# Which queue begins the store of a batch's normalised rows: from the sync engine to GpSimd, in a decoder layer on one core

## The chip, the cores and the metric

One core of one Trainium2 chip. The metric is the device time of one execution in microseconds (us), median of the runs. The engines are TensorE (PE, with its weight loads as PEld), VectorE (DVE), ScalarE (ACT), GpSimd (POOL) and the sync engine (SP), which here only begins transfers. SPq and POOLq are the queues of transfers that SP and POOL begin.

## What is computed

A post-norm decoder layer in fp32 on x of 16 batches x 256 rows x 256 columns, with a context of 77 rows per batch:

```python
x = _layernorm(x + attn(x))               # a gated scan over the rows, 16 states
x = _layernorm(x + xattn(ctx_1024, x))    # cross attention, 8 heads of 128, keys = 77 context rows + 256 latents
x = _layernorm(x + ffn(x))                # 8 experts, top 2, at most 512 rows each
```

In the last line a row that no expert takes is only normalised: `_layernorm(x)` of the second line's result. The kernel therefore writes, for every batch, the rows of the second line normalised once more (the tile `xo`) to the output, and the experts' part overwrites the rows that an expert has taken.

## The kernel before, in words

All fp32 products are made of three matmuls on a high and a low part (lines 632 to 634). The work has two parts. The first runs over the batches b = 0 to 15, each in eight heads h; the second runs over the 8 experts. The orders of all engines are written out by hand, one function `body(b, par, have, had, tile)` for each engine, and `bodies` (line 402) calls it sixteen times. `have` says what a body does beside the attention of batch b: "nxt" the mixer's end and the first norm of batch b+1, "prv" the second norm and routing of batch b-1, "ctx" one more tile of context rows (bodies 1, 3, ... 13), "aft" the mixer's first product of batch b+2. "prv" is in the bodies 1 to 15, "nxt" in 0 to 14.

What is around the change, by engine:

- GpSimd, lines 2241 to 2333. In every head it scales the softmax's rows (`prob`, line 2250, two instructions, which wait for `rinv` of VectorE, line 1867) and copies a strip of them (2253). TensorE then transposes them (line 661). At h = 0 it scatters rows of the batch before to their slots, four indirect transfers (line 2135). At h = 3 it computes `c_rs`, `xrow` and, in lines 2277 to 2280, `xo`, after a wait that the last store of `xo` has landed (`xo_st`). At h = 4 it computes `a_rs` (`powers`, line 2157), at h = 5 the first norm of the next batch (`normalised`, 2175 and 2179), at h = 6 `latents_part` (2165, 2167), at h = 6 and 7 the routing.
- VectorE, after `a_rs`, makes `lnp` (line 1576, two instructions), which TensorE transposes (line 764).
- SP, lines 534 to 575. Its queue is strictly in order. A body loads `xts` and `xs` (539, 542), then half of the values of batch b (491 to 494), context tiles, keys, then half of the values of batch b+1 after a wait for head 3 (line 563), and last the store of `xo` (line 575), after a wait for `xo_set` (574), which line 2279 raises. The next body's loads of `xts` and `xs` stand right behind it.
- After the bodies SP loads expert weights and rows, and both SP (583) and GpSimd (2352) wait once more that all 15 stores have landed.

`xo` has one buffer, [128, 2, 256] in fp32, 256 KB; a store of it has 256 rows of 1 KB.

Of the kernel before, what the change touches and what calls it, by code (L numbers as in the profile page):

```python
# [78 lines left out]
def need(eng, sem, value):  # L79

    if isinstance(value, int) and value <= 0:
        return
    eng.wait_ge(sem, value)


def at(b, value):

    return isinstance(b, int) and b == value


def build(nc, x, xT, ctxt, in_w, xp_w, out_w, vecs, vec16, Wq, Wkv, Wo, bo, emb, W1, W2, out):
# [7 lines left out]
    with top:  # L99
# [3 lines left out]
        def sem(name):  # L103
            return top.enter_context(nc.semaphore(name))
# [34 lines left out]
        def s1(name, shape, dt=F32):  # L139
            return sb(name, shape, dt, one)  # L140
# [25 lines left out]
        xo = s1("xo", [P, NT, D])  # L166
# [89 lines left out]
        def weights_in(e):  # L256
# [71 lines left out]
        xb_set, cstat_set, crs_set, x2_set, xo_set, xo_st = (  # L328
            sem("xb_set"), sem("cstat_set"), sem("crs_set"), sem("x2_set"), sem("xo_set"), sem("xo_st"))
# [83 lines left out]
        def ap(t):  # L413
            return t.bitcast(F32)
# [9 lines left out]
        out_rows = out[0:NTOK, :].rearrange("(b t p) d -> b p t d", t=NT, p=P)  # L424
# [30 lines left out]
        def _(sp):  # L455
# [8 lines left out]
            def expert_weights(e):  # L464
                for part, w in enumerate((W1, W2)):
                    sp.dma_start(wraw[:, e - 1, part, :], w[e]).then_inc(ew_ld[e - 1], 16)

            def next_context(c):

                need(sp, cxn_set, c)  # L470
                sp.dma_start(cxs[:], ctxt[bass.ds(c, 1)].rearrange("o p d -> (o p) d")).then_inc(ctx_ld, 16)

            def keep_context(c):

                need(sp, cxl_set, c + 1)
                need(sp, cx_st, 32 * c)
                for d, part in zip(cx_tiles, (cx_hi, cx_lo)):
                    sp.dma_start(d[bass.ds(c, 1)].rearrange("o p k t -> (o p) k t"), ap(part[:])).then_inc(cx_st, 16)

            def keep_values(c):  # L480

                need(sp, vcl_set, 2 * c + 2)
                need(sp, vc_st, 32 * c)
                for d, part in zip(vc_tiles, (vst_hi, vst_lo)):
                    sp.dma_start(d[bass.ds(c, 1)].rearrange("o p n -> (o p) n"), ap(part[:])).then_inc(vc_st, 16)

            def values(a, half):

                c = slice(half * 512, half * 512 + 512)
                hi, lo = [d[bass.ds(a, 1)].rearrange("o t n -> (o t) n") for d in vc_rows]  # L490
                sp.dma_start(ap(v_hi[0:CTX, 2, c]), hi[:, c]).then_inc(vc_ld[half], 16)
                sp.dma_start(ap(v_hi[CTX:CTX + REST, 2, c]), lo[32:CTX, c]).then_inc(vc_ld[half], 16)
                sp.dma_start(ap(v_lo[0:CTX, 2, c]), hi[:, c]).then_inc(vc_ld[half], 16)
                sp.dma_start(ap(v_lo[96:P, 2, c]), lo[0:32, c]).then_inc(vc_ld[half], 16)
# [39 lines left out]
            def body(b, par, have, had, tile):  # L534
                a = b + 1
                if "aft" in have:
                    sp.wait_ge(in_mm, min(2 * (b + 2), 6))
                    need(sp, xTl_set, b - 1)
                    sp.dma_start(xts[:], xT_d[bass.ds(b + 2, 1)].rearrange("o p k s -> (o p) k s")).then_inc(xT_ld, 16)
                if "nxt" in have:  # L540
                    need(sp, xa_set, a)
                    sp.dma_start(xs[:], x_d[bass.ds(a, 1)].rearrange("o p t d -> (o p) t d")).then_inc(x_ld, 16)
                if at(b, B - 2):
                    sp.wait_ge(in_mm, 2 * B)
                    sp.dma_start(w1r, W1[0]).then_inc(w1r_ld, 16)
                    sp.dma_start(w2r, W2[0]).then_inc(w2r_ld, 16)
                if "att" in have:
                    need(sp, av_mm, 8 * b)
                    values(b, 1)
                if "ctx" in have:  # L550
                    next_context(tile + 1)
                    keep_context(tile)
                if "nxt" in have:
                    need(sp, cx_st, 32 * tile + 32)
                    need(sp, k_mm, 8 * b)
                    for d, part in zip(cx_rows, (kv_hi[1 - par], kv_lo[1 - par])):
                        sp.dma_start(ap(part[:, :, S:KEYS]), d[bass.ds(a, 1)].rearrange("o p k t -> (o p) k t")
                                     ).then_inc(kvc_ld, 16)
                if "ctx" in have:
                    keep_values(tile)  # L560
                if "nxt" in have:
                    need(sp, vc_st, 32 * tile + 32)
                    need(sp, av_mm, 8 * b + 4)
                    values(a, 0)
                if at(b, B - 1):
                    sp.wait_ge(v_mm, 4 * B)
                    expert_weights(3)
                    expert_weights(7)
                    sp.wait_ge(q_mm, 4 * B)
                    expert_weights(1)  # L570
                    expert_weights(5)
                if "prv" in have:
                    c = b - 1
                    need(sp, xo_set, 2 * c + 2)
                    sp.dma_start(out_rows[bass.ds(c, 1)].rearrange("o p t d -> (o p) t d"), xo[:]).then_inc(xo_st, 16)

            bodies(sp, body)


# [1539 lines left out]
        def _(pool):  # L2119
# [34 lines left out]
            def powers(a):  # L2154

                need(pool, astat_set, 6 * a + 6)
                pool.tensor_tensor(a_rs[:].rearrange("p c t -> p (c t)"),
                                   a_vv[:].rearrange("p c t -> p (c t)"), powm[:],
                                   ALU.pow).then_inc(ars_set, 1)
# [10 lines left out]
            def normalised(b, par):  # L2170

                a = b + 1
                need(pool, ars_set, a + 1)
                for t in range(NT):
                    pool.tensor_scalar(x1[1 - par][:, t, :], xa[:, t, :], a_mv[:, t, 0:1],
                                       a_rs[:, 0, t:t + 1], ALU.subtract, ALU.mult).then_inc(x1p_set, 1)
                need(pool, x1p_set, 2 * a + 2)
                need(pool, cvec_set, 1)
                pool.tensor_tensor(x1[1 - par][:], x1[1 - par][:],
                                   cvec[:].unsqueeze(1).broadcast_to([P, NT, D]),  # L2180
                                   ALU.add).then_inc(x1_set, 1)
# [59 lines left out]
            def body(b, par, have, had, tile):  # L2241
                for h in range(H):
# [37 lines left out]
                                               ALU.add, ALU.mult).then_inc(xo_set, 1)  # L2280
                    if h == 4 and "nxt" in have:
                        powers(a)
                    if h == 5 and "nxt" in have:
                        normalised(b, par)
                    if h == 6 and "prv" in have:
# [22 lines left out]
                    if h == 7 and "prv" in have:  # L2308
# [24 lines left out]
                        pool.tensor_copy(slot_u[:], slot_a[:].rearrange("p t c -> p (t c)")).then_inc(slot_set, 1)  # L2333

            bodies(pool, body)
            ending()

# [83 lines left out]
```

## Time and profile before

| | us |
|---|---|
| median of 3 runs | 1010.71 (1010.63 to 1012.13) |
| profiled execution, its own time | 1010.28 |
| its span, first to last instruction | 1008.5 |
| PE busy | 980.1 (97%) |
| DVE busy | 828.8 (82%) |
| ACT busy | 727.9 (72%) |
| POOL busy | 578.4 (57%) |
| mean granted TensorE clock | 0.994 |

Outside the span lie 1.8 us. A row of the timeline view is: start, duration, engine, line, operation, output<-input, how many instructions it merges, and in brackets the idle time of the engine before it and who ended it. A row of the groups view ends in busy us, mean ns of one, idle us before the group with what ended it.

### The profile page before, as it was taken

What the parts mean: (1) busy time and instruction counts of PE and PEld (TensorE: products, weight loads), DVE (VectorE), ACT (ScalarE), POOL (GpSimd) and SP (SyncE); (2) the same over time, 40 slices, a digit from 0 to 9 for tenths busy, and PEclk for the clock granted to TensorE, in tenths of its full rate; (3) what the DMA queues carried; (4) which work ended last, traced back from release to release, by engine and by line L of the source; (5) the groups of instructions that cost most, each with busy time, mean ns of one, the idle gap of its engine ahead of it and who ended that gap; (6) DMA issues with size and microseconds to landing.
All of it is one profiled execution on the core that took longest, in us unless ns stands there. A gap on an engine that the chain in (4) does not pass through costs nothing.

```text
span 1008.5 us, 21673 instructions
## 1 busy us (share of the span) xinstructions
PE 980.1 (97%) x7018; PEld 928.1 (92%) x7018; DVE 828.8 (82%) x2115; ACT 727.9 (72%) x1869; POOL 578.4 (57%) x1060
## 2 busy tenths in 40 slices
PE   8999999999999999999999999999999999999994
PEld 6789999999999999999999999999999999898993
DVE  6887878888888888887888788878888887678885
ACT  6686877777787768786778677867777676546772
POOL 4743565665565656655574647565665464535775
PEclk9999999999999999999999999999999999999997
DMA  7663031112211131104110311131112303555542
GB/s 249 194 144 108 17 110 48 52 46 75 82 52 46 46 111 52 47 15 142 47 45 7 122 35 62 36 110 48 51 46 74 116 30 125 187 168 160 171 156 98
DMA packets 63030, 88.97 MB, mean 88 GB/s; under 512 B 15540, under 2 KB 44008, under 8 KB 62920
## 3 DMA queue, kind: packets, MB, share of 16 engines
q1 hardware_dynamic: 56968, 71.10, 22.9%
q0 software_dynamic: 5952, 16.50, 4.7%
q8 instruction: 58, 0.95, 0.4%
q14 instruction: 52, 0.43, 0.1%
HBM read 49.31 MB, written 38.26 MB: 87 GB/s over the span
## 4 chain that ended last, share of the span: by engine, by line
PE 79%; ACT 7%; DVE 6%; issue 4%; POOL 2%; DMA 2%; POOLq 0%; SPq 0%; DVEq 0%; ACTq 0%
PE ps L632 21%; PE ps L634 21%; PE ps L633 20%; PE ps L661 7%; PE ps L740 3%; PE ps L676 1%; PE ps L678 1%; ACT prob L1255 1%; DVE nmx L1858 1%; PE ps L778 1%; ACT hp L1098 1%; PE ps L771 1%; POOL out L2359 1%; PE ps L764 1%; DMA cxs<-in_ctxt 1%
## 5 line engine op out<-in xcount | busy, mean ns | idle before, releaser
L2250 POOL TENSOR_SCALAR prob<-prob,rinv 128x333 f32<-128x333 f32 x256 | 143.6, 572 | 235.4 <-DVE rinv L1867 234.8
L1250 ACT ACTIVATE oT_hi<-ps 128x256 fp32r<-128x256 f32 x126 | 48.3, 383 | 150.7 <-PE ps L678 150.7
L632 PE MATMUL ps<-kv_lo,w_hi 128*128 128x256 f32 (+1 forms) x512 | 154.8, 302 | 1.1 <-DVE kv_lo L1416 1.1
L634 PE MATMUL ps<-kv_hi,w_hi 128*128 128x256 f32 (+1 forms) x512 | 152.9, 299 | 0.0
L633 PE MATMUL ps<-kv_hi,w_lo 128*128 128x256 f32 (+1 forms) x512 | 152.5, 298 | 0.0
L1255 ACT ACTIVATE prob<-ps,nmx 128x333 f32<-128x333 f32 x256 | 134.8, 537 | 7.7 <-DVE nmx L1858 7.7
L1416 DVE TENSOR_TENSOR pT_lo<-ps,pT_hi 128x512 fp32r<-128x512 f32 x254 | 130.9, 548 | 0.9 <-ACT pT_hi L1267 0.3
L1858 DVE TENSOR_REDUCE nmx<-ps 128x2 f32<-128x666 f32 x128 | 108.3, 846 | 8.8 <-PE ps L634 7.5
L661 PE MATMUL ps<-ident,prob 128*128 128x128 f32 (+1 forms) x768 | 105.7, 273 | 1.8 <-POOL prob L2250 1.0
L632 PEld LDWEIGHTS ps<-kv_lo,w_hi 128*128 128x128 f32 x512 | 96.9, 189 | 1.7 <-issue 1.5
L634 PEld LDWEIGHTS ps<-kv_hi,w_hi 128*128 128x128 f32 x512 | 96.8, 189 | 0.0
L633 PEld LDWEIGHTS ps<-kv_hi,w_lo 128*128 128x128 f32 x512 | 96.5, 188 | 0.0
L661 PEld LDWEIGHTS ps<-ident,prob 128*128 128x128 f32 (+1 forms) x768 | 89.9, 140 | 6.7 <-issue 1.6
L1477 DVE SCALAR_TENSOR_TENSOR cv<-hp,vec,cv 128x256 f32<-128x256 f32 x192 | 87.5, 474 | 1.0 <-ACT cv L1146 0.9
L632 PE MATMUL ps<-k_lo,q_hi 128*128 128x334 f32 x256 | 81.2, 317 | 2.0 <-DVE k_lo L1422 2.0
L1422 DVE SCALAR_TENSOR_TENSOR k_lo<-ps,vec,k_hi 128x334 fp32r<-128x334 f32 x128 | 71.4, 558 | 12.0 <-ACT k_hi L1077 11.5
L633 PE MATMUL ps<-k_hi,q_lo 128*128 128x334 f32 x256 | 80.6, 315 | 0.0
L634 PE MATMUL ps<-k_hi,q_hi 128*128 128x334 f32 x256 | 80.4, 314 | 0.0
L632 PE MATMUL ps<-w_lo,oT_hi 128*128 128x256 f32 x254 | 77.5, 305 | 0.2 <-DVE oT_lo L1416 0.2
L1267 ACT ACTIVATE pT_hi<-ps 128x512 fp32r<-128x512 f32 x127 | 76.9, 606 | 0.4
L2135 POOL DMA_INDIRECT slots<-xrow,slot_u x60 | 63.7, 1062 | 21.7 <-issue 20.4
L1430 DVE SCALAR_TENSOR_TENSOR q_lo<-ps,vec,q_hi 128x256 fp32r<-128x256 f32 x128 | 55.8, 477 | 24.3 <-ACT q_hi L1085 24.3
(336 smaller groups left out, 3318.2 us busy)
## 6 DMA issues: line engine op xcount, KB each, us to landing
wraw<-in_W SPq DMA_DIRECT2D x14, 512.0 KB, 5.2
vcd_hi<-vst_hi SPq DMA_DIRECT2D x10, 512.0 KB, 2.7
vcd_lo<-vst_lo SPq DMA_DIRECT2D x10, 512.0 KB, 3.5
v_hi<-vcd_hi SPq DMA_DIRECT2D x32, 154.0 KB
v_lo<-vcd_hi SPq DMA_DIRECT2D x32, 154.0 KB
slots<-initr SPq DMA_DIRECT2D x8, 522.0 KB, 9.8
xs<-in_x SPq DMA_DIRECT2D x16, 256.0 KB, 4.2
xts<-in_xT SPq DMA_DIRECT2D x15, 256.0 KB, 3.9
```

Source lines behind the costliest of these rows:

```text
L632: pe.matmul(dst, hi1, lo2, start=first, stop=False, skip_group_check=True)
L633: pe.matmul(dst, lo1, hi2, start=False, stop=False, skip_group_check=True)
L634: return pe.matmul(dst, hi1, hi2, start=False, stop=last, skip_group_check=True)
L661: last = pe.transpose(ps[0:r, far if j == 2 else T0, (j % 2) * S + t * P:(j % 2) * S + t * P + P], prob[:, ring, t, j * P:j * P + r], iden ...
L1255: act.activation(prob[:, h % 2, t, 0:KEYS], ps[:, S0 + t, 0:KEYS], ACT.Exp, bias=nmx[:, h % 2, t:t + 1], accum_out=rsum[:, h % 2, t:t + 1] ...
L1267: act.activation(pT_hi[:, 0:2, :].rearrange("p j s -> p (j s)"), ps[:, T0, :], ACT.Copy).then_inc(pTh_set, 1)
L1416: return dve.tensor_tensor(dst, src, ap(hi), ALU.subtract)
L1422: dve.scalar_tensor_tensor(out=k_lo[:, idx % 2, :], in0=g[:, 0:KCOL], scalar=vec[:, V_BK + idx:V_BK + idx + 1], in1=ap(k_hi[:, idx % 2, :] ...
L1477: op = dve.scalar_tensor_tensor(out=cv[:, ct, :], in0=hp[:, ct, k:k + S], scalar=w, in1=cv[:, ct, :], op0=ALU.mult, op1=ALU.add)
L1858: dve.tensor_reduce(nmx[:, h % 2, :], ps[:, S0:S0 + NT, 0:KEYS], AX.X, ALU.max, negate=True).then_inc(nmx_set, 1)
L2135: pool.indirect_dma_start(slots, bass.IndirectOffsetOnAxis(slot_u[:, 2 * t + c:2 * t + c + 1], 0), rows[:, t, :], None).then_inc(sc_done, 16)
L2250: pool.tensor_scalar(prob[:, h % 2, t, 0:KEYS], prob[:, h % 2, t, 0:KEYS], rinv[:, h % 2, t:t + 1], 1.0, ALU.mult, ALU.mult).then_inc(norm ...
```

## The change

GpSimd's body gets the wait and the store at h = 4, behind `powers(a)` and ahead of head 5; SP's body loses both. The tile, the destination, the semaphores and the condition ("prv") stay the same.

```diff
@@ sync, end of body
-                if "prv" in have:
-                    c = b - 1
-                    need(sp, xo_set, 2 * c + 2)
-                    sp.dma_start(out_rows[bass.ds(c, 1)].rearrange("o p t d -> (o p) t d"), xo[:]).then_inc(xo_st, 16)
@@ gpsimd, body
                     if h == 4 and "nxt" in have:
                         powers(a)
+                    if h == 4 and "prv" in have:
+                        need(pool, xo_set, 2 * b)
+                        pool.dma_start(out_rows[bass.ds(b - 1, 1)].rearrange("o p t d -> (o p) t d"), xo[:]
+                                       ).then_inc(xo_st, 16)
                     if h == 5 and "nxt" in have:
                         normalised(b, par)
```

## Rows read from the trace of the kernel before

**Rows 1.** The page: busy time of each engine, and the chain by engine.

```profile
PE 980.1 (97%) x7018; PEld 928.1 (92%) x7018; DVE 828.8 (82%) x2115; ACT 727.9 (72%) x1869; POOL 578.4 (57%) x1060
...
PE 79%; ACT 7%; DVE 6%; issue 4%; POOL 2%; DMA 2%; POOLq 0%; SPq 0%; DVEq 0%; ACTq 0%
```

**Rows 2.** The stretch of bodies 2 to 14: busy us by engine, granted clock.

```profile
150.00:820.00 670.00, 668.11 (x4880) 640.30 (x4879) 568.83 (x1427) 505.57 (x1349) 393.09 (x776) 1.00 0.20 62
```

**Rows 3.** The store's own rows: issue in ns (min/median/max), and landing.

```profile
L575 SPq DMA_DIRECT2D out<-xo x15: 423/424/453, 143.6 to 863.7; - x15
...
DMA to landing us min/median/max: 3.2/3.6/6.7
```

**Rows 4.** Timeline of SP's queue, end of body 7 and of body 8.

```profile
463.85 0.45 SPq L575 DMA_DIRECT2D out<-xo  x1
464.41 0.40 SPq L539 DMA_DIRECT2D xts<-in_xT  x1
...
500.35 0.42 SPq L575 DMA_DIRECT2D out<-xo  x1
```

**Rows 5.** Timeline of GpSimd, scatters and heads 3 to 5 of body 8.

```profile
468.97 1.14 POOL L2135 DMA_INDIRECT slots<-xrow,slot_u  x1 [0.46 <-issue]
...
471.97 0.96 POOL L2135 DMA_INDIRECT slots<-xrow,slot_u  x1 [0.30 <-issue]
...
490.75 1.09 POOL L2279 TENSOR_SCALAR xo<-xb,c_nm,c_rs 128x256 f32<-128x256 f32 x2
...
497.52 1.02 POOL L2157 TENSOR_TENSOR a_rs<-a_vv,powm 128x4 f32<-128x4 f32 x1 [3.43 <-DVE a_vv L1568]
500.87 1.22 POOL L2250 TENSOR_SCALAR prob<-prob,rinv 128x333 f32<-128x333 f32 x2 [2.33 <-DVE rinv L1867]
502.15 0.26 POOL L2253 COPY prob<-prob 128x90 f32<-128x90 f32 x1
```

**Rows 6.** Timelines of ScalarE and VectorE, first readers of xts and xs.

```profile
476.39 0.62 ACT L1138 ACTIVATE xt_hi<-xts 128x512 fp32r<-128x512 f32 x1
...
495.47 0.69 DVE L1556 TENSOR_TENSOR xa<-ps,xs 128x512 f32<-128x512 f32 x1 [0.39 <-PE ps L746]
```

**Rows 7.** Scatters and lnp: ns min/median/max.

```profile
L2135 POOL DMA_INDIRECT slots<-xrow,slot_u x60: 956/970/1262, 150.3 to 883.3; - x60
...
L1576 DVE TENSOR_SCALAR lnp<-xa,a_mv,a_rs x32: 401/406/823, 28.1 to 817.4; 128x256 f32<-128x256 f32 x32
```

**Rows 8.** Timeline of GpSimd, body 14 and body 15 (heads 4, 5).

```profile
815.40 1.02 POOL L2157 TENSOR_TENSOR a_rs<-a_vv,powm 128x4 f32<-128x4 f32 x1 [2.95 <-DVE a_vv L1568]
818.33 1.07 POOL L2250 TENSOR_SCALAR prob<-prob,rinv 128x333 f32<-128x333 f32 x2 [1.91 <-DVE rinv L1867]
...
861.96 0.26 POOL L2253 COPY prob<-prob 128x90 f32<-128x90 f32 x1
866.66 1.06 POOL L2250 TENSOR_SCALAR prob<-prob,rinv 128x333 f32<-128x333 f32 x2 [4.44 <-DVE rinv L1867]
```

**Rows 9.** Timeline of TensorE: transposes of head 5's prob, and of lnp.

```profile
504.97 0.82 PE L661 MATMUL ps<-ident,prob 128*128 128x128 f32 x6
...
500.89 0.51 PEld L764 LDWEIGHTS ps<-ident,lnp 128*128 128x128 f32 x4
```

**Rows 10.** Timelines of VectorE and GpSimd, three places where both work.

```profile
28.08 1.15 DVE L1576 TENSOR_SCALAR lnp<-xa,a_mv,a_rs 128x256 f32<-128x256 f32 x2
...
28.24 0.83 POOL L2152 TENSOR_TENSOR cx_lo<-cfull,cx_hi 128x256 fp32r<-128x256 f32 x1 [0.35 <-DVE cx_hi L1518]
...
472.18 0.48 DVE L1477 SCALAR_TENSOR_TENSOR cv<-hp,vec,cv 128x256 f32<-128x256 f32 x1
...
499.96 0.73 DVE L1576 TENSOR_SCALAR lnp<-xa,a_mv,a_rs 128x256 f32<-128x256 f32 x2
...
921.04 0.16 DVE L1895 CAST tku<-xsl 128x8 uint32<-128x8 f32 x1
...
920.92 1.08 POOL L2359 DMA_INDIRECT out<-fo,tku  x1 [1.71 <-ACT fo L1363]
```

## Prediction

> **What bounds the kernel.** I read the page's busy row and its chain first. TensorE is busy 97% of the span, GpSimd 57%; the queues SPq and POOLq hold 0% of the chain, and transfers 2% [rows 1]. Then the stretch in which 13 of the 15 moved stores lie: from 150 to 820 us TensorE is busy 668.11 of 670.00 us at the full granted clock [rows 2]. So in the batches TensorE's own work sets the end, all its idle time together is below 2 us, and no shorter path on another engine can give back more than that. Third, the timelines of the two queues that trade the instruction, and of the engines that wait behind them. The question is only whether GpSimd, once it carries the store, makes TensorE late somewhere.
>
> **What is removed.** SP begins 15 stores at 0.42 us each, 6.3 us in all; they need 3.6 us to land at the median, 6.7 us at most [rows 3]. Ahead of the store SP stands in no wait for xo: in body 8 its store starts at 500.35 us [rows 4], and xo was written by 491.84 us [rows 5], 8.5 us earlier. What stands behind it, the loads of xts and xs, starts 0.56 us after it (463.85 to 464.41) [rows 4] and can come about that much earlier. The load of xts from 464.41 us is first read by ScalarE at 476.39 us, 12 us later, and that of xs, right behind it, by VectorE at 495.47 us, 31 us later [rows 6]. An earlier start changes neither, and TensorE has nearly no idle time to give back. Gain: 0.
>
> **What is added.** Fifteen times GpSimd gets one wait and one transfer at head 4, behind a_rs. The wait is for its own xo, written at 491.84 us; a_rs ends at 498.54 us [rows 5], so it never holds. No plain transfer is begun by GpSimd in this trace, so its price is bounded from both sides. The nearest rows are its indirect ones: 0.97 us at the median for a scatter of 128 rows of about the same length, 0.96 to 1.26 us [rows 7]. From below: 0.42 us, which SP takes for the very same transfer [rows 3]. From above: a moved store has 256 rows of 1 KB where a scatter has 128; if the whole time went by rows it would be 2 x 0.97 = 1.94 us. I take 1.1 us, near the scatters, because it is the same engine and the same sort of work, and because no index has to be read. Ahead of it comes a gap of 0.30 to 0.46 us, as ahead of the scatters [rows 5]. Together 1.4 to 1.6 us, ends 0.7 and 2.4 us.
>
> **What hides it.** In body 8 GpSimd stands idle for 2.33 us between a_rs and the scaling of head 5, since rinv of VectorE comes only then [rows 5]. The same place reads 2.29 to 2.65 us in each of the bodies 1 to 13; in body 14 it is 1.91 us [rows 8], and in body 15, which has no a_rs, the store comes behind the copy that ends at 862.22 us and the next head starts 4.44 us later [rows 8]. So 1.4 to 1.6 us fit everywhere, and the upper end of 2.4 us would push head 5 back by 0.1 us (0.5 us in body 14). Even that costs nothing: head 5's prob is done at 502.41 us, and TensorE takes it up at 504.97 us [rows 5, 9], 2.56 us later. If this cover were gone, GpSimd would be the late engine and each further us would cost up to 15 us in all. Term: 0.
>
> **What follows it.** With the store begun near 498.9 us instead of 500.35 us (in bodies with a context tile, such as 7, near 444.5 instead of 463.85 us) the landing comes earlier too. Its only waiters are GpSimd before the next xo, over 35 us later, and the two waits after the bodies. The software queue now carries the store ahead of the next scatters, which in the next body come over 20 us after it: no queueing. The four transfers of values that SP begins at the same time in even bodies share the transfer engines with it as before, and no wait of TensorE is ended by one of them. In body 15 SP's next instructions wait for the last keys anyway. The tail after 905 us, where POOL transfers are on the chain, holds no moved store. Term: 0.
>
> **The place that is tight.** VectorE's lnp reads what a_rs made and starts at 499.96 us; it ends at 500.69 us [rows 10], and TensorE's weight load for its transposes starts at 500.89 us [rows 9]: 0.20 us of slack, the smallest on the way. lnp can be held by GpSimd: of its 32 instructions 31 take about 0.41 us and one takes 0.82 us [rows 7], the second of the pair at 28.08 us, beside GpSimd's cx_lo, which began before it [rows 10]. If a running transfer instruction held it in the same way, what counts is when that ends. With the gap of 0.30 us and 1.1 us it ends at 499.94 us, just ahead of lnp; with 0.46 us and 1.26 us at 500.26 us, lnp would be done at 500.99 us and TensorE 0.10 us late. What speaks against any hold: in this trace VectorE works unslowed while a GpSimd transfer instruction runs. The cast at 921.04 us takes 0.16 us inside a scatter that began at 920.92 us, and cv, which began at 472.18 us inside a scatter, takes 0.48 us [rows 5, 10], its usual time. I take 0.
>
> The Trainium skill has a rule against this change: its page "SBUF — State Buffer", section "Who interferes with whom", says that GpSimd shares its ports with VectorE, that the first to begin keeps them for its whole instruction, and that descriptors made by GpSimd are held up by VectorE's two-port operations where those of the sync queue are not. The trace agrees for arithmetic (0.82 us against 0.41 us) and shows no hold between a transfer instruction and the small cast. By that rule the change would cost what the first rival gives, by the bounds without it 0.
>
> **Sum.** 1010.28 us of the profiled execution, minus 0, plus 0 = 1010.3 us. The median of the runs lies 0.4 us above that execution, so I write 1010.6 us for the median to come.
>
> **Rivals.**
> First, slower: lnp held by the store's instruction, in bodies 1 to 14. It decides once that instruction ends later than 500.16 us, in other words once it lasts longer than 1.2 to 1.3 us. At the upper price of 1.94 us it ends at 500.78 us with the short gap; lnp is 0.82 us late, less 0.20 us of slack makes 0.62 us of TensorE per body, 13 bodies 8.1 us, and about 1 us in body 14, where a_rs ends at 816.42 us [rows 8] and VectorE comes to lnp sooner: 1019 to 1020 us. At 1.5 us it is 0.2 us per body, 1013 us. For it: lnp has been held once, and the transfer has twice the rows of a scatter. Against it: the two VectorE instructions above. Chance 0.13.
> Second, faster: SP's loads come 0.5 us earlier, the values' loads no longer share their moment with a store in the context bodies, and the late waits of TensorE shrink. All its idle time from 150 to 820 us is 1.9 us, so even a full success gives 1008.7 us, within 0.2%; beyond that only if the page hides a wait. Chance 0.06.
> Third, it does not do what it says: the store does not come off the late place on SP but lands just as late, because in bodies without a context tile it moves by only 1.5 us. Then nothing differs anywhere: 1010.6 us. That is not to be told from my forecast by the time, and is part of its chance.
>
> **How the numbers follow.** One measurement of this kernel can tell about 0.2%, 2.0 us, from no change. My forecast with the third rival has 0.81, the held lnp 0.13, the faster case 0.06. The held lnp below 0.15 us per body stays within 0.2% and is in the 0.81. The range takes the forecast's own scatter, 1010.6 to 1012.1 us in the three runs shown, downwards the 1 us that half of TensorE's idle time would give, and upwards the first rival up to the 1.5 us transfer: 1009.5 to 1013.2 us.
>
> **What would show it.** In the profile after: GpSimd has 15 plain transfers of 0.9 to 1.3 us that begin 0.3 to 0.5 us after a_rs; its idle time in front of head 5's scaling falls from 2.3 to below 1 us while that scaling still starts at rinv; its busy time grows by some 16 us to 595 us and TensorE's stays at 980 us. lnp keeps its 0.41 us, and TensorE shows no new wait for it. The prediction is wrong if that transfer takes near 2 us, if lnp reads 0.6 us or more, or if TensorE waits for lnp or prob once per body.

## The result, and the profile after

| | us | interval or runs |
|---|---|---|
| kernel before, median | 1011.39 | 1010.09 to 1012.53, 12 runs |
| changed kernel, median | 1013.84 | 1012.23 to 1016.06, 12 runs |
| ratio | 1.0025 | 1.0018 to 1.0033 |
| changed kernel, profiled execution | 1014.39 | its span 1012.4 |

The change makes the kernel slower by a quarter of a per cent, some 2.5 us: more than the 0.2% that count as no change. The median of 1013.84 us lies above the predicted range, which ended at 1013.2 us.

The page of the changed kernel, against [rows 1]: busy time by engine, and the chain.

```profile
PE 981.9 (97%) x7018; PEld 929.3 (92%) x7018; DVE 826.9 (82%) x2115; ACT 729.0 (72%) x1869; POOL 592.9 (59%) x1075
...
PE 78%; ACT 7%; DVE 6%; issue 4%; POOL 2%; DMA 2%; POOLq 0%; SPq 0%; DVEq 0%; ACTq 0%
```

GpSimd has 15 instructions and 14.5 us more, as it must. Nothing else stands out, and the chain still gives the queues 0%. The two lines that one reads first don't show the loss.

The same stretch as in [rows 2], bodies 2 to 14, of the changed kernel: us, then busy time of PE, PEld, DVE, ACT and POOL, granted clock, share of the transfer engines, GB/s.

```profile
150.00:820.00 670.00, 668.20 (x4876) 640.22 (x4876) 565.83 (x1424) 505.79 (x1348) 405.41 (x789) 1.00 0.19 61
```

TensorE is busy 668.20 of 670 us against 668.11 before. 13 of the 15 moved stores lie here, and they cost it nothing.

The moved store's own rows in the changed kernel (ns: min/median/max; then us from issue to landing), against [rows 3].

```profile
L2281 POOL DMA_DIRECT2D out<-xo x15: 841/862/982, 126.6 to 863.9; - x15
...
DMA to landing us min/median/max: 2.7/3.5/6.0
```

The timeline of GpSimd, heads 3 to 5 of body 8, changed kernel, against [rows 5].

```profile
498.91 1.02 POOL L2153 TENSOR_TENSOR a_rs<-a_vv,powm 128x4 f32<-128x4 f32 x1 [3.43 <-DVE a_vv L1564]
499.90 0.86 POOL L2281 DMA_DIRECT2D out<-xo  x1
502.26 1.21 POOL L2246 TENSOR_SCALAR prob<-prob,rinv 128x333 f32<-128x333 f32 x2 [1.50 <-DVE rinv L1863]
```

The store stands straight behind `a_rs`, with no gap, and takes 0.86 us where SP took 0.42. The idle time ahead of head 5's scaling falls from 2.33 to 1.50 us, and the scaling still starts at `rinv`. VectorE's `lnp`, for which the prediction saw a risk, is as before [rows 7]:

```profile
L1572 DVE TENSOR_SCALAR lnp<-xa,a_mv,a_rs x32: 404/407/819, 29.4 to 819.1; 128x256 f32<-128x256 f32 x32
```

So where are the 2.5 us? Compare the ends. Line 99 holds the instructions that close each engine's program. These are some of them in the kernel before (ns: min/median/max, then the first and last start in us).

```profile
L99 POOLq EVENT_SEMAPHORE  x2: 17/17/17, 1008.4 to 1008.4; - x2
...
L99 DVEq DRAIN  x1: 786/786/786, 1001.0 to 1001.0; - x1
L99 POOLq DRAIN  x1: 6378/6378/6378, 1001.9 to 1001.9; - x1
L99 SPq COMPARE_BRANCH  x1: 38/38/38, 1007.7 to 1007.7; - x1
```

And in the changed kernel:

```profile
L99 POOLq EVENT_SEMAPHORE  x2: 17/17/17, 1012.2 to 1012.2; - x2
...
L99 DVEq DRAIN  x1: 772/772/772, 1001.3 to 1001.3; - x1
L99 POOLq DRAIN  x1: 9880/9880/9880, 1002.2 to 1002.2; - x1
L99 SPq COMPARE_BRANCH  x1: 38/38/38, 1008.0 to 1008.0; - x1
```

SP leaves its last wait, for the landing of the last output rows, by 1007.7 and 1008.0 us: up to there the two kernels are 0.3 us apart. But the program ends when GpSimd's DRAIN does (its closing instruction, called the drain below), and that takes 9.88 us instead of 6.38. The DRAIN is recorded beside the last transfer instructions, so the useful number is how long after the last of them it ends. Here is the end of GpSimd's timeline, before:

```profile
987.96 0.99 POOL L2346 DMA_INDIRECT bs<-slots,tku  x1 [1.41 <-DMA slots<-yo]
991.08 0.98 POOL L2346 DMA_INDIRECT bs<-slots,tku  x1 [2.13 <-issue]
...
1005.22 0.97 POOL L2359 DMA_INDIRECT out<-fo,tku  x1 [0.30 <-issue]
```

and in the changed kernel:

```profile
990.09 0.99 POOL L2346 DMA_INDIRECT bs<-slots,tku  x1 [1.67 <-DMA slots<-yo]
991.38 0.97 POOL L2346 DMA_INDIRECT bs<-slots,tku  x1 [0.30 <-ACT fo L1359]
...
1005.51 0.97 POOL L2359 DMA_INDIRECT out<-fo,tku  x1 [0.30 <-issue]
```

Before, the last one ends at 1006.19 us and the DRAIN 2.1 us later; after, at 1006.48 us and the DRAIN 5.6 us later. This time from the end of the last transfer instruction to the end of the drain, worked out in the same way for every run below, is called **the drain's tail**. It grows by 3.5 us.

Something is given back. In the kernel before, GpSimd stands 2.13 us ahead of the second gather for the last expert (line 2346) although nothing that the profile shows holds it; in the changed kernel that **gap** is 0.30 us, as between the gathers behind it. These 1.83 us come back in full: from the first of these gathers to the last transfer it is 17.26 us before (987.96 to 1005.22) and 15.42 us in the changed kernel (990.09 to 1005.51). Sum: 3.5 - 1.8 = 1.7 us at the end. The other 2.1 us of the 3.8 us between the ends of the two drains were lost ahead of that gather, and most of them at the start: the first `lnp` comes 1.3 us later (29.4 against 28.1 us), the last one 1.7 us later (819.1 against 817.4 us). In the first 50 us TensorE's granted clock is 0.97 in this one execution of the changed kernel and 1.00 in that of before.

```profile
0.00:50.00 50.00, 43.32 (x227) 36.00 (x228) 36.29 (x89) 32.86 (x66) 28.94 (x42) 0.97 0.66 214
```

The same source run once more (e2) has 1.00 there, its first `lnp` at 28.1 us, and a span of 1009.5 us. The start varies from execution to execution whatever the kernel does with its stores: in e11 below, which has no such store at all, the first `lnp` comes at 30.7 us.

### The profile page after: what moved, and what is told of

The parts are those of the page before. It is cut to its first block, busy times and chain, and to the rows that moved or that the text cites. A ratio compares the mean times of both kernels' runs of the same rounds, so it can differ in the third digit from the quotient of the medians.

```text
span 1012.4 us, 21673 instructions
## 1 busy us (share of the span) xinstructions
PE 981.9 (97%) x7018; PEld 929.3 (92%) x7018; DVE 826.9 (82%) x2115; ACT 729.0 (72%) x1869; POOL 592.9 (59%) x1075
## 4 chain that ended last, share of the span: by engine, by line
PE 78%; ACT 7%; DVE 6%; issue 4%; POOL 2%; DMA 2%; POOLq 0%; SPq 0%; DVEq 0%; ACTq 0%
PE ps L628 21%; PE ps L630 20%; PE ps L629 20%; PE ps L657 7%; PE ps L736 3%; PE ps L672 1%; PE ps L674 1%; DVE nmx L1854 1%; ACT prob L1251 1%; PE ps L774 1%; ACT hp L1094 1%; POOL out L2359 1%; PE ps L767 1%; PE ps L760 1%; DMA cxs<-in_ctxt 1%
```

## The experiments

The drain's tail and the gap are read in every trace as above, the tail to the nanosecond. The runs e5 to e8 fell on another chip, where the kernel before has 1024.44 us; they are not in the table, and all others are compared with a kernel before of 1010.8 to 1011.3 us on their own chip. "Blocks" counts GpSimd's transfers beyond those of the kernel before in blocks of 128 rows; a store of `xo` has two.

| run | GpSimd does besides | blocks | gap us | tail us | ratio (95% interval) |
|---|---|---|---|---|---|
| e1, e9 | nothing (kernel before) | 0 | 2.13 | 2.1 | 0.9996 (0.9984 to 1.0007), 0.9994 (0.9984 to 1.0003) |
| e11 | nothing, stores left out | 0 | 2.13 | 2.1 | 1.0005 (0.9995 to 1.0014) |
| e13 | 60 memsets | 0 | 2.13 | 2.2 | 0.9998 (0.9989 to 1.0008) |
| e3 | 1 store | 2 | 2.14 | 2.1 | 0.9999 (0.9989 to 1.0009) |
| e18 | 2 stores | 4 | 0.30 | 1.9 | 0.9981 (0.9971 to 0.9992) |
| e14 | 4 stores | 8 | 0.30 | 9.2 | 1.0053 (1.0036 to 1.0070) |
| e15 | 8 stores | 16 | 0.30 | 7.9 | 1.0042 (1.0025 to 1.0059) |
| e16 | 11 stores | 22 | 0.30 | 6.9 | 1.0045 (1.0028 to 1.0062) |
| e12 | 26 indirect transfers | 26 | 0.30 | 6.0 | 1.0023 (1.0013 to 1.0032) |
| e2 | 15 stores (changed kernel) | 30 | 0.30 | 5.6 | 1.0016 (1.0006 to 1.0026) |
| e4 | 15 stores as 30 | 30 | 0.31 | 5.6 | 1.0015 (1.0006 to 1.0024) |
| e10 | 15 more, SP keeps its own | 30 | 0.31 | 5.6 | 1.0018 (1.0009 to 1.0028) |
| e17 | 25 stores, 10 for nothing | 50 | 0.30 | 7.7 | 1.0037 (1.0023 to 1.0050) |

### e1 and e2: both kernels once more

No edit. 

> The kernel before, once more, as the null measurement. In the first traces GpSimd's closing DRAIN took 6.38 us before and 9.88 us after the change, and the bodies differed by only 0.45 us. Theory E (end): the loss is in that closing drain, so this run shows 6.3 to 6.5 us again and a ratio of 1.000. Rival S (scatter of single executions): the drain varies from run to run whatever the kernel, and this one may read 9 us as well. Rival L (loop): the loss is in the bodies; nothing is said of the drain.

> The changed kernel, once more. Theory E: the closing drain of GpSimd is 9.7 to 10.0 us again, 3.5 us over the kernel before, the last transfer of GpSimd ends less than 0.7 us later than before's does, ratio 1.002 to 1.004. Rival S: drain anywhere from 6.3 to 10 us, ratio still above 1 for another reason. Rival L: the start of the last body is over 2 us later than in e1 at equal clocks, drain not decisive.

Measured: 1010.91 and 1012.52 us beside 1011.07 of the kernel before on that chip. Gap and tail are as in the first traces, each to 0.1 us.

```profile
L99 POOLq DRAIN  x1: 9802/9802/9802, 999.5 to 999.5; - x1
```

So the longer drain belongs to the kernel and not to one execution, and so does a loss of 1.5 to 2.5 us.

### e3: one store alone

```diff
+ON_POOL = (1,)
-                if "prv" in have:
+                if "prv" in have and b not in ON_POOL:
...
+                    if h == 4 and "prv" in have and b in ON_POOL:
+                        need(pool, xo_set, 2 * b)
+                        pool.dma_start(out_rows[bass.ds(b - 1, 1)].rearrange("o p t d -> (o p) t d"), xo[:]
+                                       ).then_inc(xp_st, 16)
```

> Only body 1's store is begun by GpSimd (with a completion semaphore of its own), the other 14 by SP as before. Theory E in its fixed form (a single plain transfer on GpSimd is enough): the drain is 9.9 us and the time 2 to 3.5 us above before, ratio 1.0025. Theory E in its counted form (so much for each transfer or descriptor, 3.5/15 = 0.23 us each): drain 6.6 us, ratio 1.000 to 1.001. Rival L: ratio 1.0002, a fifteenth of the loss.

Measured: 1011.00 us, gap and tail of the kernel before.

```profile
L107 POOLq DRAIN  x1: 6312/6312/6312, 1002.4 to 1002.4; - x1
```

It is not enough that GpSimd has a plain transfer at all.

### e4: fifteen stores as thirty transfers

```diff
-                        pool.dma_start(out_rows[bass.ds(b - 1, 1)].rearrange("o p t d -> (o p) t d"), xo[:]
-                                       ).then_inc(xo_st, 16)
+                        for t in range(NT):
+                            pool.dma_start(out_rows[b - 1][:, t, :], xo[:, t, :]).then_inc(xo_st, 16)
```

> Every store is cut into two transfers of 128 rows on GpSimd, 30 instead of 15, the same rows in all. Fixed form: drain 9.9 us, as with 15. Counted by transfers: 6.4 + 7.0 = 13.4 us, ratio 1.006. Counted by rows: 9.9 us. Rival L: each body has two transfer instructions of about 0.85 us and a gap, 2.0 us of the 2.33 us idle time; if bodies lose, they now lose twice as much, ratio 1.005, with the drain unchanged from 15.

Measured: 1013.15 us, tail 5.6 us: twice the instructions and the same rows give the same tail. At this amount the number of instructions plays no part. The halves take 18.7 us of GpSimd together where the whole ones took 15 x 0.86 = 12.9 us, and that costs nothing either:

```profile
L2282 POOL DMA_DIRECT2D out<-xo x30 | 18.7, 625 | 0.1
```

### e5 to e8: on another chip

e5, e6 and e7 give GpSimd the stores of bodies 1 to 4, 1 to 8 and 1 to 11 (`ON_POOL` longer); e8 leaves the stores on SP and repeats GpSimd's four scatters in seven bodies, at h = 0, into a spare tensor.

> The stores of bodies 1 to 4 by GpSimd, the other 11 by SP. GpSimd's closing DRAIN ends 2.1 us after its last transfer instruction with 0 stores and with 1, and 5.6 us after it with 15. Threshold theory (the step of 3.5 us comes once enough descriptors or transfers have gone through GpSimd's queue): 2.1 us here, unless the threshold is very low. Linear theory (0.23 us for each store, which one store would have hidden in its scatter): 3.0 us. Plain-transfer theory (from the second on): 5.6 us.

> The stores of bodies 1 to 8 by GpSimd, 7 by SP. Threshold theory: 2.1 or 5.6 us and nothing between; linear theory: 4.0 us. The idle gap of 2.13 us that the kernel before shows ahead of the second gather for the last expert, and that 15 or 30 stores do not show, should go together with the short drain: gap and 2.1 us, or no gap and 5.6 us, if both are one event that the number of transfers ahead of it moves.

> The stores of bodies 1 to 11 by GpSimd, 4 by SP. Threshold theory: 2.1 or 5.6 us, with e6 a bracket for the threshold; linear theory: 4.7 us.

> The kernel before, all stores by SP, and in bodies 3 to 9 the four scatters are done once more, into a spare tensor: 28 more indirect transfers on GpSimd, 3584 rows, as the 15 stores have 3840. If it is the count of descriptors or transfers on GpSimd's queue, whatever their kind: the closing drain ends 5.6 us after the last transfer instruction, the gap of 2.13 us is gone. If it is plain transfers: 2.1 us and the gap as in the kernel before. About 5 us more of GpSimd's time at head 0 of seven bodies may cost the bodies something; the drain is what is asked.

Measured: 1032.68 us (one run), 1032.75 (ratio 1.0074, 1.0050 to 1.0099), 1032.28 (one run) and 1063.65 (1.0382, 1.0338 to 1.0426). With no trace of the kernel before on this chip the times of e5 to e7 can't be taken apart (e6 loses 8.3 us here, and the same kernel as e15 4.3 us on its chip), but their tails can be read: 9.2, 7.9 and 6.9 us, not the two levels that I had looked for. These are to 0.01 us what another chip gave later for the same kernels. The tail of e8 is 7.6 us for 28 blocks.

e8 lost its time elsewhere. The 28 scatters take 27.0 us and stand behind 8.5 us of gaps, 35.5 us in all. From the first `lnp` to the last, which spans the batches, e8 takes 822.4 us and e5 789.6 us:

```profile
L1579 DVE TENSOR_SCALAR lnp<-xa,a_mv,a_rs x32: 406/410/828, 27.4 to 849.8; 128x256 f32<-128x256 f32 x32
```

```profile
L1585 DVE TENSOR_SCALAR lnp<-xa,a_mv,a_rs x32: 405/408/821, 29.7 to 819.3; 128x256 f32<-128x256 f32 x32
```

So at h = 0 some nine tenths of GpSimd's added time are paid. The 15 stores lie at h = 4, where it stands idle. The place decides, as the prediction had it.

### e9 to e12: what counts is what GpSimd transfers

e9 is the kernel before. e10 leaves the stores on SP and lets GpSimd store `xo` once more at the place of the change, into a spare tensor. e11 leaves out the 15 stores of the normalised rows (so these rows are missing in its output) and all waits for them. e12 leaves SP's stores and adds 26 indirect transfers of 128 rows at h = 4. The diffs are those of e10, e11 and e12.

```diff
+                    if h == 4 and "prv" in have:
+                        need(pool, xo_set, 2 * b)
+                        pool.dma_start(spare_rows[b - 1], xo[:]).then_inc(xp_st, 16)
```

```diff
-                if "prv" in have:
-                    c = b - 1
-                    need(sp, xo_set, 2 * c + 2)
-                    sp.dma_start(out_rows[bass.ds(c, 1)].rearrange("o p t d -> (o p) t d"), xo[:]).then_inc(xo_st, 16)
```

```diff
+                    if h == 4 and "prv" in have and 1 < b < B - 1:
+                        need(pool, xo_set, 2 * b)
+                        for t in range(NT):
+                            pool.indirect_dma_start(
+                                spare, bass.IndirectOffsetOnAxis(slot_u[:, 2 * t:2 * t + 1], 0),
+                                xo[:, t, :], None).then_inc(xp_st, 16)
```

> The kernel before, unchanged, so that the closing DRAIN of GpSimd has its baseline on this chip. e5 to e8 ran on another chip than e1 to e4, on which the kernel before takes 1024 us instead of 1011 us, and their drains of 6.9 to 9.2 us after the last transfer instruction have no baseline. On a chip like the first: drain 2.1 us after the last transfer instruction, gap of 2.13 us ahead of the second gather of the last expert. Every theory says so; if it varies here, the drain is no steady quantity and rival S gains.

> SP keeps its 15 stores, and GpSimd begins 15 plain ones of the same tile at the place of the change, into a spare tensor. SP's instructions stand where they stood in the kernel before. Theory E, by GpSimd's transfers: drain 3.5 us longer than in e9, gap gone, ratio 1.0015 to 1.0025. Rival P (place: what changed the drain is that SP's queue has 15 instructions fewer, so that its code is fetched at other moments): drain and gap as in e9, ratio 1.000.

> The 15 stores of xo are left out on both engines, with the waits for their landing. Theory E: drain and gap as in e9, ratio 0.999 to 1.000, since the stores cost SP and the transfer engines nothing that the bodies wait for. Rival P: the drain 3.5 us longer as in the changed kernel.

> SP keeps its 15 stores; GpSimd begins 26 more indirect transfers of 128 rows of xo into a spare tensor, two at head 4 of bodies 2 to 14: 150 transfers, 19200 rows in all, against 139 and 19712 in the changed kernel. Theory E by amount of transfers or rows, whatever their kind: drain 3.5 us longer than in e9 and the gap gone. Theory E by kind (plain transfers only): drain and gap as in e9. The bodies have room for 2.5 us more of GpSimd at head 4, with at most 0.2 us of its delay passed on.

Measured: e9 1010.35, e10 1012.85, e11 1011.05, e12 1013.17 us. The line of e10's drain, and that of e11's:

```profile
L100 POOLq DRAIN  x1: 9232/9232/9232, 1000.8 to 1000.8; - x1
```

```profile
L99 POOLq DRAIN  x1: 6298/6298/6298, 1006.6 to 1006.6; - x1
```

e10 has the whole loss although SP does all that it did before; e11 takes the stores from SP, gives them to nobody, and loses and gains nothing that its interval can tell. So what is taken from SP plays no part of that size. e12 shows that indirect transfers do it too.

### e13 to e16: code, or amount?

An engine's added instructions move all its later code, and a stall for code might fall elsewhere. e13 adds 60 memsets of one column, each with a wait, and no transfer. e14, e15 and e16 are e5, e6 and e7 on a chip where the kernel before has 1011.25 us.

```diff
+                    if h == 4 and "prv" in have:
+                        for i in range(4 * (b - 1), 4 * b):
+                            need(pool, idle_set, i)
+                            pool.memset(idle1[:], 0.0).then_inc(idle_set, 1)
```

> The kernel before, to which GpSimd gets 60 small memsets of one column (four in each of bodies 1 to 15, where the change has its store), each behind a wait of its own, so 120 instructions more and no transfer more. Theory T (the number of transfers that GpSimd has begun decides): the closing DRAIN stays at 6.2 to 6.4 us and ends 2.1 us after the last transfer instruction, the idle 2.13 us ahead of the last expert's second gather stays, the ratio is 1.000 (0.999 to 1.001). Rival C (the place of GpSimd's code behind the added instructions decides, so that a stall for code falls elsewhere): the 2.13 us go and the DRAIN grows to 9 to 10 us, as in the changed kernel, or both move to other places; the ratio is then 1.0015 to 1.0025.

> GpSimd begins the stores of bodies 1 to 4 alone (128 transfers of its own instead of 124), the sync engine those of bodies 5 to 15. Here on the chip of the short times, if the kernel before shows about 1011 us. Theory T: a step between 1 and 15 more. If it lies below 5 the DRAIN ends 5.6 us after the last transfer instruction and the ratio is 1.0015 to 1.0025, if above it 2.1 us and 1.000. If the two parts (the idle 2.13 us, the longer DRAIN) do not step at the same count, a kernel between has the first gone and the second short, and is 1.6 to 2.1 us faster than the kernel before (0.998).

> The same with the stores of bodies 1 to 8 on GpSimd (132 transfers). As for four: DRAIN end at 2.1 or 5.6 us behind the last transfer instruction, and the ratio 1.000 or 1.0015 to 1.0025 by it; 0.998 if only the idle 2.13 us has gone. If the DRAIN grew with every transfer, by 3.5/15 us each, it would end at 2.1 + 8 x 0.23 = 4.0 us here and at 3.1 us for four.

> The same with the stores of bodies 1 to 11 on GpSimd (135 transfers). By a step: 2.1 or 5.6 us; by growth with each transfer 2.1 + 11 x 0.23 = 4.7 us. Ratio 1.000 with the short DRAIN, 1.0015 to 1.0025 with the long one, 0.998 if only the idle 2.13 us has gone.

Measured: 1011.55, 1016.50, 1015.52 and 1015.72 us. e13, of 60 memsets and 120 instructions more:

```profile
991.41 0.98 POOL L2352 DMA_INDIRECT bs<-slots,tku  x1 [2.13 <-issue]
```

```profile
L99 POOLq DRAIN  x1: 6455/6455/6455, 1002.3 to 1002.3; - x1
```

Gap and tail stay where they were: the account by code falls, as far as 120 instructions can show it. e14's drain, and e15's:

```profile
L107 POOLq DRAIN  x1: 13505/13505/13505, 1000.6 to 1000.6; - x1
```

```profile
L107 POOLq DRAIN  x1: 12142/12142/12142, 1000.9 to 1000.9; - x1
```

The tail does not grow with the amount. It jumps above 9 us and then falls: 9.23, 7.92, 6.95 and 5.64 us at 8, 16, 22 and 30 blocks, that is 1.31 us for 8 blocks, 0.97 for 6 and 1.31 for 8, close to a straight line of 0.163 us a block. Four stores on GpSimd cost at least twice as much as all fifteen (5.3 us against 1.5 to 2.5 us). Both of my expectations (a level, growth with each transfer) were wrong.

### e17 and e18: where the line goes, and a faster kernel

e17 is the changed kernel with ten more stores behind the moved ones, into a spare tensor; e18 is e3 with the stores of bodies 1 and 2.

```diff
+                        if b <= 10:
+                            pool.dma_start(spare_rows[b - 1], xo[:]).then_inc(xp_st, 16)
```

```diff
+ON_POOL = (1, 2)
```

> The changed kernel, with ten more plain stores of xo by GpSimd into a spare tensor in bodies 1 to 10, behind the real ones: 50 blocks of 128 rows more than in the kernel before. The runs with 8, 16, 22 and 30 blocks more have the end of the DRAIN 9.23, 7.92, 6.95 and 5.64 us behind the last transfer instruction, which is a line that falls by 0.163 us a block. Theory L (the line goes on: the DRAIN works off what is left of something that is used up in proportion to the rows moved): 5.64 - 20 x 0.163 = 2.38 us with 50 blocks, and the idle 2.13 us ahead of the last expert's second gather is still gone. The kernel is then faster than the changed one by 3.2 us and than the kernel before by 1.3 to 1.9 us (ratio 0.998 to 0.999), although it moves 2.5 MB more for nothing. Rival F (the DRAIN has a few fixed levels, or rises again with more transfers): it stays at 5.64 us or more, and the ratio is 1.0015 to 1.003, since the extra stores save nothing.

> GpSimd begins the stores of bodies 1 and 2 alone, 4 blocks of 128 rows more than the kernel before. With 2 blocks more the trace is that of before (2.12 us, the gap of 2.13 us in place), with 8 more the gap is gone and the DRAIN ends at 9.23 us. Theory L with the jump between 2 and 4: the line gives 9.23 + 4 x 0.163 = 9.88 us and a ratio of 1.006; with the jump between 4 and 8: 2.12 us, the gap in place, ratio 1.000. Rival F: one of the levels seen, 9.23 or 2.12 us.

e17 measured 1014.47 us: the line doesn't go on to 2.4 us.

```profile
L100 POOLq DRAIN  x1: 11807/11807/11807, 1000.2 to 1000.2; - x1
```

Its last transfer instruction ends at 1004.36 us and the tail is 7.7 us. So between 30 and 50 blocks the tail rises again. It may be a sawtooth; two rises are seen, the second only between these two counts.

e18 measured 1009.03 us, ratio 0.9981 (0.9971 to 0.9992), from 8 runs. The end of its timeline and its drain:

```profile
988.13 0.99 POOL L2359 DMA_INDIRECT bs<-slots,tku  x1 [1.72 <-DMA slots<-yo]
989.42 0.97 POOL L2359 DMA_INDIRECT bs<-slots,tku  x1 [0.30 <-issue]
...
1003.65 0.97 POOL L2372 DMA_INDIRECT out<-fo,tku  x1 [0.30 <-issue]
```

```profile
L107 POOLq DRAIN  x1: 5997/5997/5997, 1000.5 to 1000.5; - x1
```

Here the gap is gone, and the drain stays short. The last transfer instruction ends 1.57 us earlier than before (1004.62 against 1006.19) and the tail is 0.25 us shorter (1.87 against 2.12), together 1.8 us; 1.7 us is what the medians show (1009.03 against 1010.77). It beats both kernels. With two blocks less nothing is gained and with four more some 7 us are lost, so this is a lucky place and not a design.

**The bookkeeping.** By tail and gap alone a kernel should lose what its tail has grown by, less 1.8 us where the gap is gone. Beside the differences of the medians that gives, in us: e14 5.3, measured 5.3; e17 3.7 and 3.7; e15 4.0 and 4.3; e12 2.0 and 2.3; e4 and e10 1.7, and 2.1 and 2.0; e2 1.7 and 1.5; e18 -2.1 and -1.7. The first measurement of the changed kernel is 0.8 us above its sum (1.7 and 2.5), and e16 1.5 us above (3.0 and 4.5). What e16 loses beyond the drain was not tested. Its trace has it behind the batches: from the first output of an expert to the last it is 83.7 us there (921.6 to 1005.3) and 82.6 us in e15 (921.5 to 1004.1).

Nothing of size is lost in the batches themselves: from the first `lnp` to the last it is 789.2 to 789.9 us in all 16 traces on the chips of the short times, with 0 to 25 stores or 26 indirect transfers more on GpSimd.

## Why the prediction was wrong, point by point

- **What bounds the kernel** was right for the batches: TensorE stays at 668 of 670 us from 150 to 820 us.
- **What is removed: 0.** Right within 0.1%, and shown by e11: without any of these stores the time is 1.0005 (0.9995 to 1.0014) of before.
- **The price of the store.** 1.1 us was taken between 0.42 and 1.94; it is 0.86 us, less than a scatter of half the rows, and the gap of 0.30 to 0.46 us that I added is absent behind `a_rs`. Together 0.9 us instead of 1.4 to 1.6. The rows had more to say here. Where a transfer instruction of GpSimd begins early in VectorE's `w_lo`, which reads two tiles, it takes 1.83 to 1.86 us (four of them in the trace of before) and ends some 0.85 us after `w_lo` does. Two of the four:

```profile
923.36 1.22 DVE L1416 TENSOR_TENSOR w_lo<-wraw,w_hi 128x1024 fp32r<-128x1024 f32 x1 [0.25 <-ACT w_hi L1163]
923.60 1.83 POOL L2359 DMA_INDIRECT out<-fo,tku  x1 [0.30 <-issue]
...
935.48 1.22 DVE L1416 TENSOR_TENSOR w_lo<-wraw,w_hi 128x1024 fp32r<-128x1024 f32 x1 [0.26 <-ACT w_hi L1163]
935.69 1.86 POOL L2359 DMA_INDIRECT out<-fo,tku  x1 [0.30 <-issue]
```

  In 14 of the 15 bodies the moved store begins inside VectorE's `nmx` instead, which reads TensorE's result, and it takes 0.84 to 0.98 us. In body 8 of the changed kernel the store begins at 499.90 us, inside the `nmx` shown below. So the small price may belong to this place; whether a plain store begun inside `w_lo` would be held too, no run shows.

```profile
499.52 0.84 DVE L1854 TENSOR_REDUCE nmx<-ps 128x2 f32<-128x666 f32 x1
```

- **What hides it.** Right: the idle time ahead of head 5 falls from 2.33 to 1.50 us in body 8, and even the 18.7 us of e4 leave the batches alone. e8 shows that the same sort of work at h = 0 costs nine tenths of itself.
- **The tight place.** The first rival, to which I gave 0.13, didn't come; its time of 1013 us at a 1.5 us transfer resembles the result by chance only. The changed kernel alone hardly tests it: in the bodies 1 to 13 the store ends 0.5 to 0.9 us before `lnp` starts, which has its usual 0.41 us. e12 and e17 do test it. In e17 ten `lnp` begin inside the second store and take 0.40 to 0.41 us, and in e12 fifteen begin inside an indirect transfer and take no longer. One place of e17:

```profile
444.79 0.74 POOL L2289 DMA_DIRECT2D spare<-xo  x1
444.95 0.48 DVE L1477 SCALAR_TENSOR_TENSOR cv<-hp,vec,cv 128x256 f32<-128x256 f32 x1
445.34 0.73 DVE L1576 TENSOR_SCALAR lnp<-xa,a_mv,a_rs 128x256 f32<-128x256 f32 x2
```

  The two VectorE instructions that ran unslowed inside a transfer instruction were the right evidence. The Trainium skill's rule ("SBUF — State Buffer", "Who interferes with whom") would have cost what that rival gives. These traces show no `lnp` held by a transfer instruction. The other way round, with VectorE first and GpSimd's transfer instruction behind it, the rows of `w_lo` above agree that the first to begin goes on and the other waits.
- **The step that failed** is the one on what follows: "The tail after 905 us, where POOL transfers are on the chain, holds no moved store. Term: 0." The term is about +2 us (-1.8 for the gap, +3.5 for the drain's tail). No moved store lies there, but GpSimd's drain ends the program, and its length hangs on what GpSimd has transferred before, even 140 us before (the last store begins at 863.9 us) and long landed; in e14 the last of GpSimd's four stores begins at 286.3 us, some 700 us before the end. I had read the page's chain (POOLq 0%) and never the closing instructions, where before the change 2.1 us already stood between the last transfer instruction and the end, some 0.6 us of them after SP had left its wait for the landing (1007.7 us, and the drain ends at 1008.3 us). What I could have seen is that the drain is the last thing to end and belongs to the engine that gets the work. How long it would become was in no row of that trace.
- **The chances.** "Slower" had 0.13, all of it for a mechanism that is absent. A rival "something of GpSimd's own at the end of the program grows" was missing. None of the signs that the prediction had set for being wrong came (a transfer near 2 us, `lnp` at 0.6 us, a wait of TensorE in every body): they all looked at the batches, where nothing was lost.

**What is shown and what is not.** Shown: the loss is in the drain of GpSimd (e2, e4, e10); it needs GpSimd's transfers (e10, e11, e13), plain or indirect (e12); at 30 blocks it is the same for 15 and for 30 instructions with the same rows (e4); it is not monotone (e14 to e18). What sets its length is open. A guess is that the drain works off the rest of something that the transfers use up in proportion to their rows and that starts anew when it is used up: a straight fall of 0.163 us a block with a rise now and then would fit. It was not tested, and three facts don't follow from it alone: the flat 2.1 us and the gap at 0 and 2 blocks, the 6.0 us of e12 where the line gives 5.64 + 4 x 0.163 = 6.3, and e8's 7.6 us at 28 blocks, where it gives 6.0. What makes the gap of 2.13 us is open too; it is absent in every traced kernel with 4 blocks or more.

## What to carry to other kernels

Read the closing instructions of each engine as well as the chain and the busy rows: if GpSimd's drain ends the program, transfers given to GpSimd can move the end by microseconds, in either direction, even where they lie over 100 us ahead of it. Try two or three neighbouring amounts of GpSimd transfers before judging such a change, since 4, 8 and 30 blocks gave -1.7, +5.3 and about +2 us. And the cover that was worked out from idle time in one head did hold: a 0.86 us instruction in a 2.3 us hole costs nothing, where nine tenths of the same sort of work at h = 0 are paid.

## What the runs showed of the hardware that was not expected

- GpSimd's closing drain ends 1.9 to 9.2 us after its last transfer instruction, though SP's wait for the landing of that transfer is over 1.4 to 1.6 us after it in every trace. The time changes with what GpSimd has transferred in the whole program, and repeats to about 0.01 us in another chip's run of the same kernel.
- An indirect transfer instruction of GpSimd that begins early in VectorE's `w_lo` (1.22 us, two tiles read) takes 1.83 to 1.86 us in the kernel before, instead of 0.97; a `lnp` of VectorE that begins inside a transfer instruction of GpSimd keeps its 0.41 us (e12, e17).
- GpSimd begins a plain transfer of 256 rows of 1 KB in 0.86 us, and one of 128 rows in 0.63 us (18.7 us for 30); the indirect one of 128 rows takes 0.97 us, SP's of 256 rows 0.42 us. The landing takes the same on both queues: 3.5 us here, 3.6 us from SP [rows 3].
- One chip is 1.3% slower than the others with the same kernel (1024.44 against 1010.8 to 1011.3 us). Not its batches: e5 to e7 take 789.6 to 790.9 us for them there. The experts' part is what is longer: from the first gather to the last transfer instruction 103.6 us in e5 (916.7 to 1020.3) and 89.0 us in e14 (914.9 to 1003.9), the same kernel. Why is open.
